# Attention of a convolution and attention hybrid: operands as two float32r parts in the two row halves of the array, and maxima over 1024 columns

## What is computed

```python
# 1: attention with 8 heads of 8 channels, output projection, group norm, residual
q, k, v = x_seq @ W.T + bias            # (2, 8 heads, 1024, 8)
attn = softmax(einsum('bhnd,bhmd->bhnm', q, k) * 8 ** -0.5)
out = einsum('bhnm,bhmd->bhnd', attn, v) @ Wo.T + bo
x = group_norm(out) * gn_w + gn_b + x
# 2: t += four layers of eight heads of linear attention on layer_norm(t)
# 3: t += mixture of 8 experts, the two likeliest of each token, on layer_norm(t)
```

## Time and profile before

| | us |
|---|---|
| median of 3 runs | 305.08 |
| lowest and highest | 303.81, 306.98 |
| span of the profiled execution | 304.2 |

### The profile page before, as it was taken

The page is one execution under the profiler, slowest core; times in us unless marked ns, Lnnn a source line. Parts: engine busy times, 40 slices in busy tenths (PEclk is TensorE's granted clock), DMA queues, the critical chain, the costliest instruction groups (busy, mean ns, idle before and its releaser), DMA issues.

```text
span 304.2 us, 6027 instructions
## 1 busy us (share of the span) xinstructions
PE 288.6 (95%) x2349; PEld 138.7 (46%) x2350; DVE 217.1 (71%) x449; ACT 189.0 (62%) x347; POOL 44.8 (15%) x92
## 2 busy tenths in 40 slices
PE   7998899998999999999999999999998998898995
PEld 5643334443444444444444444444444885567221
DVE  4699999887888888888888888888212663258432
ACT  2646657776677787777778777786887231139210
POOL 9486321101010010100201011010100000000421
PEclk9999999999999999999999999999999999999999
DMA  6565000555205000000000000000000000000001
GB/s 208 197 143 125 1 2 13 203 117 146 60 6 210 2 3 4 3 1 4 0 4 0 4 3 3 5 0 4 2 2 1 2 0 2 0 2 1 0 33 38
DMA packets 6186, 11.81 MB, mean 39 GB/s; under 512 B 1938, under 2 KB 3546, under 8 KB 5594
## 3 DMA queue, kind: packets, MB, share of 16 engines
q1 hardware_dynamic: 6156, 11.42, 13.3%
HBM read 8.18 MB, written 3.23 MB: 38 GB/s over the span
## 4 chain that ended last, share of the span: by engine, by line
PE 80%; DVE 12%; DMA 3%; issue 1%; ACT 1%; SPq 0%; DVEq 0%
PE psum L446 22%; PE psum L431 21%; PE psum L389 15%; DVE negmax_half L863 7%; PE psum L615 5%; PE psum L319 2%; DMA max_scratch<-max_row 2%; PE psum L346 2%; PE psum L601 2%; PE psum L530 1%; PE psum L408 1%; PE psum L539 1%; DMA wqk_sb<-in_wqk 1%; PE psum L455 1%; PE psum L464 1%
## 5 line engine op out<-in xcount | busy, mean ns | idle before, releaser
L863 DVE TENSOR_REDUCE negmax_half<-psum 128x1 f32<-128x512 f32 x256 | 163.2, 686 | 26.7 <-PE psum L389 24.6
L748 ACT ACTIVATE probs<-psum 128x512 f32<-128x512 f32 x256 | 149.8, 598 | 51.2 <-PE psum L431 50.6
L431 PE MATMUL psum<-qop,kop 99*128 99x256 bf16 x512 | 96.8, 274 | 1.6 <-DMA qop<-max_scratch 1.2
L446 PE MATMUL psum<-probs,v_aug 128*32 128x256 f32 x1024 | 81.3, 391 | 0.0
L389 PE MATMUL psum<-kop,qop 96*128 96x512 bf16 x256 | 77.8, 380 | 1.9 <-DVE negmax_half L863 1.2
L431 PEld LDWEIGHTS psum<-qop,kop 99*128 99x128 bf16 x512 | 39.8, 97 | 75.0 <-ACT probs L748 36.4
L446 PEld LDWEIGHTS psum<-probs,v_aug 128*32 128x32 f32 x1024 | 20.6, 108 | 26.1 <-issue 24.5
L389 PEld LDWEIGHTS psum<-kop,qop 96*128 96x128 bf16 x256 | 23.9, 98 | 17.0 <-DVE negmax_half L863 11.8
L654 POOL CAST max_part<-negmax 128x8 bf16<-128x8 f32 x16 | 3.1, 191 | 167.2 <-issue 159.1
L691 POOL TENSOR_TENSOR qop<-probs,qop 128x512 f32<-128x512 f32 x5 | 6.3, 1269 | 76.6 <-ACT probs L821 76.6
L455 PE MATMUL psum<-cbf_sb 128*128 128x256 bf16 x124 | 14.8, 272 | 0.0
(11 more groups left out here) (159 smaller groups left out, 196.1 us busy)
## 6 DMA issues: line engine op xcount, KB each, us to landing
parts_scratch<-part SPq DMA_DIRECT2D x10, 256.0 KB, 2.9
qop<-parts_scratch SPq DMA_DIRECT2D x9, 192.0 KB
kop<-parts_scratch SPq DMA_DIRECT2D x9, 192.0 KB
vt_sb<-in_vt SPq DMA_DIRECT2D x1, 1024.0 KB, 4.8
sel_sb<-in_sel SPq DMA_DIRECT2D x1, 576.0 KB, 5.7
x_sb<-in_x SPq DMA_DIRECT2D x1, 512.0 KB, 3.3
q_pair<-in_q_pairs SPq DMA_DIRECT2D x1, 512.0 KB, 5.6
qop<-parts_scratch SPq DMA_DIRECT2D x3, 144.0 KB
```

Of the source, the lines that this page charges most:

```text
L431: last = nc.tensor.matmul(psum[:, ST_BANKS[s % len(ST_BANKS)], i * QB:(i + 1) * QB], kop[0:SCORE_ROWS, b, h, mt * P:(mt + 1) * P], qop[0:S ...
L446: last = nc.tensor.matmul(psum[j * VW:(j + 1) * VW, PV_BANK, 0:QB], v_aug[:, mt, b, g * HG + j, :], probs[:, u % P_RING, j, :], start=mt = ...
L748: nc.scalar.activation(probs[:, u % P_RING, 2 * pair:2 * pair + 2, :], psum[:, ST_BANKS[s % len(ST_BANKS)], :].rearrange("p (i n) -> p i n ...
L863: V.tensor_reduce(negmax_half[:, i, c, k:k + 1], psum[:, bank, :], AX_X, ALU.max, negate=True).then_inc(S["slot_free"], 1)
```

## The change

- An operand is split into two float32r parts, not three bf16 ones. A head has 4 combinations x 8 channels = 32 rows and 2 rows for the maximum, 34 in all. Two heads lie in one tensor, one from row 0, the other from row 64.
- A block is one image, 2 heads and 512 queries (still 16 blocks of 8 steps). `scores` is one matmul per head, 34 rows by 512 queries. The maxima use the same rows with the maximum's rows in them (`fill` has put zeros into `qop` and ones into `kop`), one matmul per head over 512 keys; DVE reduces both heads' banks, 1024 columns, at once.
- A slot is a pair of banks, 0 and 1 or 2 and 3. The step's order is: scores of head 0, maxima of head 1, values, scores of head 1, maxima of head 0, small jobs.
- `values` has the same shapes; its four strips are 2 heads x 2 quarters of the queries.
- Selection matmuls and `sel` are gone. Operands of the first pair of heads are made by f32 matmuls with replicated weights (`w_rep`), and two parts are formed by ScalarE and DVE (the last chunk by GpSimd), with small tables that GpSimd, PE and DVE make first. Split on GpSimd is two operations, not four. Rows of maxima of block 0 come from f32 matmuls.
- The other operands go through DRAM as f32, 16 DMAs a group. A row of maxima takes two DMAs, not one. `project(1)` and the second `attn_t` piece come after the last step.

The core of the diff:

```diff
-BLOCKS = [(b, g, qb) for b in range(B) for g in range(NG) for qb in range(N // QB)]
+PP = H // 2
+BLOCKS = [(b, pp, qh) for b in range(B) for pp in range(PP) for qh in range(HALVES)]
...
+SPLIT = 2
+COMBOS = SPLIT * SPLIT
+HEAD_AT = 64
+TOP_ROW = COMBOS * DH
+SCORE_ROWS = TOP_ROW + SPLIT
...
-        qop = sb("qop", [P, B, H, N], BF16)
-        kop = sb("kop", [P, B, H, N], BF16)
+        qop = sb("qop", [P, B * PP, N], F32R)
+        kop = sb("kop", [P, B * PP, N], F32R)
...
-        slot_bank = [r % 4 if r <= LAST_MAX else 2 * (r % 2) for r in range(len(SLOT_JOBS))]
+        def slot_bank(r):
+            return 2 * (r % 2)
...
+                for w, (op, part_of) in enumerate(((qop, Q_PART), (kop, K_PART))):
+                    for i in range(2):
+                        for r in range(COMBOS):
+                            at = HEAD_AT * i + DH * r
+                            sp.dma_start(op[at:at + DH, b * PP + first:b * PP + end, :].bitcast(F32),
+                                         rows[part_of[r], w, i, :, first:end, :]).then_inc(ops_in[g], 16)
...
+            for i, (what, hf) in enumerate(CHUNKS):
+                pe.wait_ge(S[f"in_x{hf}"], 16)
+                nc.tensor.matmul(psum[:, 4 + i, :], w_rep[:, int(what == "k"), :], x_sb[:, hf * NH:(hf + 1) * NH],
+                                 start=True, stop=True).then_inc(S["rep_full"], 1)
...
+            def max_scores(job, h):
+                kind, blk, k, _ = job
+                r = slot[0]
+                b, pp, qh = BLOCKS[blk]
+                t, c = divmod(k, HALVES)
+                if r >= 2:
+                    pe.wait_ge(S["slot_free"], r - 1)
+                at = slice(HEAD_AT * h, HEAD_AT * h + SCORE_ROWS)
+                return nc.tensor.matmul(psum[:, slot_bank(r) + h, :],
+                                        qop[at, b * PP + pp, qh * NH + t * P:qh * NH + (t + 1) * P],
+                                        kop[at, b * PP + pp, c * NH:(c + 1) * NH], start=True, stop=True)
...
-                for i in range(2):
-                    h = g * HG + 2 * pair + i
-                    last = nc.tensor.matmul(psum[:, ST_BANKS[s % len(ST_BANKS)], i * QB:(i + 1) * QB],
-                                            kop[0:SCORE_ROWS, b, h, mt * P:(mt + 1) * P],
-                                            qop[0:SCORE_ROWS, b, h, qb * QB:(qb + 1) * QB],
-                                            start=True, stop=True, skip_group_check=True)
+                at = slice(HEAD_AT * h, HEAD_AT * h + SCORE_ROWS)
+                nc.tensor.matmul(psum[:, ST_BANKS[s % len(ST_BANKS)], :],
+                                 kop[at, b * PP + pp, mt * P:(mt + 1) * P],
+                                 qop[at, b * PP + pp, qh * NH:(qh + 1) * NH],
+                                 start=True, stop=True).then_inc(S["st_full"], 1)
...
+                top = jobs.pop(0) if jobs and jobs[0][0] == "max" else None
+                if top and u < 0:
+                    fill_slot(top)
+                    top = None
+                if top:
+                    before_max(top)
                 if 0 <= u < UNITS:
                     scores(u, 0)
+                if top:
+                    max_scores(top, 1)
                 if 0 < v - 1 < UNITS and (v - 1) % TT == 0:
                     values(v - 1)
-                for job in jobs[:HALVES]:
-                    fill_slot(job)
+                if 0 <= v < UNITS and (v == 0 or v % TT):
+                    values(v)
                 if 0 <= u < UNITS:
                     scores(u, 1)
-                for job in jobs[HALVES:]:
+                if top:
+                    max_done(max_scores(top, 0))
+                for job in jobs:
                     fill_slot(job)
...
-                    V.tensor_reduce(negmax_half[:, i, c, k:k + 1], psum[:, bank, :], AX_X, ALU.max,
+                    V.tensor_reduce(negmax_half[:, i, c, :, t], psum[:, bank:bank + 2, :], AX_X, ALU.max,
                                     negate=True).then_inc(S["slot_free"], 1)
```

More of the change, by code:

```diff
@@ L8 @@
 F32 = mybir.dt.float32
+F32R = mybir.dt.float32r
 BF16 = mybir.dt.bfloat16
@@ L60 @@
 P_RING = 8
-IN_REST = 10
+IN_REST = 11
 PROJ_BANKS = (1, 3)
@@ new lines, in max_done @@
+            def max_done(last):
+                slot[0] += 1
+                last.then_inc(S["slot_full"], 1)
+            def fill_slot(job):
+                kind, blk, k, _ = job
+                if kind == "max":
+                    before_max(job)
+                    max_scores(job, 0)
+                    max_done(max_scores(job, 1))
+                    return
+                r = slot[0]
+                bank = slot_bank(r)
+                if r >= 2:
+                    pe.wait_ge(S["slot_free"], r - 1)
+                if kind == "max_r":
+                    for h in range(2):
+                        last = rows_of_max(blk, h, bank + h)
@@ L632, in _ @@
+            for hf in range(HALVES):
+                at = slice(hf * NH, (hf + 1) * NH)
+                pool.wait_ge(S["parts0_in"], 2 * (hf + 1))
+                nc.gpsimd.tensor_tensor(part[1][:, 0, at].bitcast(F32R), rest[:, 0, at], part[0][:, 0, at],
+                                        ALU.subtract).then_inc(S["parts0"], 1)
             pool.wait_ge(S["v_out"], 2)
@@ L677, in _ @@
                     pool.wait_ge(S["parts1_in"], blk + 1)
-                    split(rest[:, 1, at], [part[s][:, 1, at] for s in range(3)], rest[:, 1, at], "parts1")
+                    link(nc.gpsimd.tensor_copy(part[0][:, 1, at].bitcast(F32R), rest[:, 1, at]))
+                    nc.gpsimd.tensor_tensor(part[1][:, 1, at].bitcast(F32R), rest[:, 1, at], part[0][:, 1, at],
+                                            ALU.subtract).then_inc(S["parts1"], 1)
+                    pool.wait_ge(S["parts1"], blk + 1)
                 if blk == 10:
@@ L855, in _ @@
-            for r, (kind, blk, k, c) in enumerate(SLOT_JOBS):
-                bank = slot_bank[r]
-                b, g, qb = BLOCKS[blk]
+            V.memset(w_rep[:], 0.0).then_inc(S["w_rep_zero"], 1)
+            V.memset(fill[:, 1, :], 1.0).then_inc(S["fill_ready"], 1)
+            dve.wait_ge(S["w_rep_zero"], 1)
+            dve.wait_ge(S["in_w"], 16)
+            for w in range(2):
+                for i in range(2):
+                    last = V.tensor_copy(w_rep[:, w, HEAD_AT * i:HEAD_AT * i + TOP_ROW].rearrange("p (r d) -> p r d", d=DH),
+                                         wqk_sb[:, 0:1, :].rearrange("p o (d v) -> p o d v", d=DH)[:, :, :, w * H + i]
+                                         .broadcast_to([P, COMBOS, DH]))
@@ L858, in _ @@
+            for r, (kind, blk, k, _) in enumerate(SLOT_JOBS):
+                bank = slot_bank(r)
+                b, pp, qh = BLOCKS[blk]
                 i = blk % 2
```

443 lines of the change are left out of this document (213 added, 230 removed).

## The result

| | before | after |
|---|---|---|
| median of four runs | 305.57 | 430.46 |
| lowest and highest | 303.81 to 306.98 | 429.13 to 432.15 |
| span of the profiled execution | 304.2 | 427.3 |
| mean granted clock of TensorE | 1.00 | 0.629 |

The changed kernel takes 1.408 times as long (95% interval 1.400 to 1.416). The forecast was 308 with a range of 288 to 334, so the time lies far outside.

A forecast was written before the change was run, and what follows sets the result against it. The prediction took TensorE, 95% busy, as the bound. To the profiled 304.2 us it added +1.0 ahead, -0.5 for first steps, +3.0 for thirteen blocks and +0.3 behind: 308.0, range 288 to 334.

The forecast's parts named there:

- one pass per float32r column: Score and maxima matmuls: 512 float32r columns take 0.216 us, the bf16 rate, with 0.43 kept as a rival.
- the overlap of the halves: Score and maxima matmuls: two heads' row halves run fully side by side, so a step costs PE 1.11 us against 1.55.
- the weight loads: Before PE's matmuls: mostly hidden behind the other half; 0.043 longer in each of four handovers, 0.17 us a block taken.
- rival C: Score and maxima matmuls: one float32r matmul takes 0.43 us, block 14.8, total 331; sign, matmuls longer than 0.40; chance 0.12.
- The block walk: Eight-step block: waits for the two pairs of PSUM banks make it 12.95 us, 13.12 with weight loads, against 12.86 now.
- two long waits in steps 4 and 5: Sign in each block: DVE idle before its reduction for about 1.5 and 1.3 us, released by PE's maxima.
- The handover of step 5: From a reduction's end to the start of the one taking over its banks: 1.35 us, 1.39 with its weight load.
- the floor of 9.9: DVE in a block: eight 1024-column reductions and four small operations take 9.9 us; as the bound, it would save 38.
- Ahead: Before the loop: first maxima at 12.5 to 13.5 us, first scores later by 1, with -1 to +4.
- A: Block's bank handovers: shorter than forecast; without mode-change costs 1.10 us, block 12.1, total 294.8; chance 0.28.
- B: Score and maxima matmuls: the two row halves do not overlap, so block 14.8 us and total 331; chance 0.11.
- D: Score and maxima matmuls: float32r runs at f32 rate, 0.85 us each, block 20.5, total over 400; chance 0.03.

The follow-up runs named there:

- 14 to 16: Changed kernel with values behind both maxima and zeros written by memsets, at 64, 48 and 34 rows a head: 292.8 to 297.5, 295.7 to 307.3, 388.4 to 405.0 us.
- experiment 2: Changed kernel with 64 rows a head instead of 34, the 30 added rows zeros moved in by four DMAs: 351.34 us.
- the best version: Changed kernel with 64 rows a head, values behind both maxima, zeros written by memsets: 296.23 us, ratio 0.966 to the kernel before.
- experiment 3: Changed kernel with each float32r matmul over 98 rows at once, no row halves, summing both heads' scores: 367.69 us.
- rows34_both: Changed kernel, still 34 rows a head, with small jobs moved to bank 6 and values behind both maxima: 361.02 us; four later executions 348.89 to 385.65.

## Why the prediction was wrong, step by step

**The missing term.** The sum costed every instruction at the durations of a kernel that ran at full clock, and no line of it asked whether that clock would stay. The change took the rows of the score matmuls from 99 and 96 to 34; nothing in the list of what is removed and added spoke of that. The runs of 14 to 16 size it: at one order, 34 rows cost 18.43 - 11.67 = 6.8 a block over 64. In the changed kernel the blocks take 265.5; at the 14.16 that its own order shows at full clock (experiment 2) they would take 184.1. So about 81 of the 123 is the clock in the blocks. Behind the last transpose it is about 12 of the 15, by the 91.2 of experiment 2. Of the 9 ahead the low clock (21 us at 0.50 before 58) must be a part, but no run says how large.

**Durations at full clock.** Of TensorE's terms, one pass per float32r column holds (0.23 to 0.24 a matmul against 0.216), and the overlap of the halves holds: the second pair takes 0.32 to the values (52.75 to 53.07), my 0.216 + 0.10. But the pair behind the values costs 0.34, not 0.216. I had let the weight loads hide behind the other half and added only 0.04 for the first one behind the values, from the f32 load of the earlier trace rows; a float32r load takes 187 ns at full clock (group mean of the run with 64 rows and memsets) for 98, so 0.09 of the surplus of 0.12 would be the load. This is the term of the sum that was mis-sized: a step is 1.23 where I had 1.11. One sign that I named for rival C was badly chosen: the float32r matmul behind the values lasts 0.49, longer than 0.40, and yet streams at one pass.

**The block walk.** Its mechanism was right: VectorE's two long waits in steps 4 and 5, released by PE's maxima, 1.86 and 1.24. The handover of step 5 is made of 0.05 for the release, 0.42 from maxima 1 to the values, 0.57 for the values and 0.57 from scores 1 to the reduction, against 0.02, 0.32, 0.58 and 0.43 in my sum: maxima 1 starts behind a wait and the last pair behind the values, and they take 0.10 and 0.14 more. Four handovers a block at 0.22 above my 1.39 give 13.12 + 0.9 = 14.0, measured 14.16. The thirteen blocks would then have added 17 where I had 3. With the rest of the sum as it stood that is about 322: slower, and inside the range, had the clock stayed.

**VectorE and ScalarE.** A reduction lasts 1.22 as worked out, and ahead of the loop the next one follows after 1.13:

```profile
14.54 2.35 DVE L912 TENSOR_REDUCE negmax_half<-psum 128x2 f32<-128x1024 f32 x2
```

In the loop of the best version PE's step of 1.23 sets the pace, so the floor of 9.9 was reached by no version: eight at 1.23 are 9.9 for PE alone, and the waits and small jobs around the two transposes add 1.7 to give 11.56.

**Ahead.** First maxima at 13.84 against 12.5 to 13.5. First scores at 30.00 where I had 28.4, inside my bounds of -1 to +4; the four projections of 3.44 in place of 1.98 are there at half clock.

**Rivals.** A (a shorter handover): no, it is longer. B and C: no. D gave a block of 20.5 and over 400. The block measured is 20.5, but D's reason, f32 rate, is refuted by experiment 3: the same number came from another cause, by luck.

**What stays open.** Why the clock, once lost, came back at about 115 in one execution of rows34_both and elsewhere in others; what full-array work does for it, since eight matmuls a step brought it back in some stretches only; how far waits of PE matter beside the rows, since at 64 rows the clock was low for 37 us of the blocks in experiment 2 and for 0 to 7 once ring or order had been changed; and whether it is the rows of the scores, of the maxima, or their sum that matters.

## What to carry to other kernels

Before an operand is packed into fewer rows, ask what the engine's clock does: at full clock a block over 34 rows takes what one over 64 takes (11.72), and here the few rows lost half the clock for 300 us. Rows of zeros, written once by an idle engine, bought most of it back. To see it in a trace, read the granted clock first and look for an unchanged instruction that has become longer.

## What the runs showed of the hardware

- **Rows and the granted clock.** PE busy for 273 of 280 us at 34 rows for each of two heads was granted 0.50; 13 blocks at 64 rows were granted 1.00 with PE busy for 141 of 151 us in the best version, while 64 rows in the order of the change (experiment 2) had 0.50 for some 37 of 196. The Trainium skill, "TensorE: Matmul & The Clock Gate", Part 1, ties the clock to how busy PE has been, and says that the throttled state is the default and activity releases it. The fall at 23 after a wait for VectorE agrees with that; the blocks do not, if busy means instructions that run, as here the busier engine had the lower clock.
- **At 34 rows it is not settled by the program.** Five executions of one program took 349 to 386, while the six of the best version at 64 rows took 293 to 297.
- **float32r**: 0.23 to 0.24 for 512 columns over 98 rows at full clock, one pass. Two row halves side by side take 0.43 at half clock where the pair follows another pair, which is 512 columns, and 0.59 behind the values; at full clock 0.34 behind the values.
- **Row halves in bf16** show no such surplus: 0.41 for a pair behind the values at half clock.
